# A transformer layer on one core: where the next chunk's residual work stands in the FFN stage

## The reference

```python
x = layernorm(x + attention(x))      # 8 heads of 64, 2 key heads, partial rotary, gated, projected by Wo
h = x @ W1.T + gate * (x @ v.T @ fast_b.T @ u.T)   # W1: ternary weights times a scale, 1024 hidden
r = relu(h)
x = layernorm(x + (r * r) @ W2.T)    # W2: ternary weights times a scale
```

## Time and profile before

| | us |
|---|---|
| median of 3 runs | 1777.85 |
| lowest, highest | 1777.14, 1778.02 |
| the profiled execution | 1775.12 |
| its span in the profile | 1773.3 |
| TensorE busy | 1670.2 (94%) |
| VectorE busy | 1390.5 (78%) |
| GpSimd busy | 989.9 (56%) |
| ScalarE busy | 742.0 (42%) |
| mean granted TensorE clock | 0.972 |

### The profile page before, as it was taken

The page is one execution under the profiler, slowest core; times in us unless marked ns, Lnnn a source line. Parts: engine busy times, 40 slices in busy tenths (PEclk is TensorE's granted clock), DMA queues, the critical chain, the costliest instruction groups (busy, mean ns, idle before and its releaser), DMA issues.

```text
span 1773.3 us, 26408 instructions
## 1 busy us (share of the span) xinstructions
PE 1670.2 (94%) x6902; PEld 817.4 (46%) x6902; DVE 1390.5 (78%) x1692; ACT 742.0 (42%) x1407; POOL 989.9 (56%) x765
## 2 busy tenths in 40 slices
PE   5699999999999999999868999999999999999996
PEld 3444444444444444447744444444444444444585
DVE  6668888888888888757766788888888888885587
ACT  1244444444444444444422444444444444445352
POOL 0546666666666665653334566666666666657342
PEclk8799999999999999999987999999999999999998
DMA  4600101000000000020043010000000000000001
GB/s 163 159 18 23 23 23 24 22 22 22 23 22 22 22 20 19 1 78 24 25 115 84 18 29 23 23 23 22 22 22 23 22 22 22 19 1 1 25 25 48
DMA packets 36916, 59.76 MB, mean 34 GB/s; under 512 B 6624, under 2 KB 17264, under 8 KB 36288
## 3 DMA queue, kind: packets, MB, share of 16 engines
q1 hardware_dynamic: 36800, 58.50, 12.6%
HBM read 20.07 MB, written 4.19 MB: 14 GB/s over the span
## 4 chain that ended last, share of the span: by engine, by line
PE 75%; DVE 10%; issue 8%; ACT 2%; DMA 2%; POOL 1%; SPq 1%; DVEq 0%; ACTq 0%; POOLq 0%
PE ob L578 24%; PE trio L566 16%; PE trio L567 11%; PE sc L533 8%; PE trio L513 6%; PE trio L672 3%; DVE acc L328 2%; PE trio L589 2%; DVE maxp L1059 2%; PE sc L639 2%; ACT probs L824 2%; DMA acc<-in_x 1%; PE ob L687 1%; PE trio L687 1%; PE trio L525 1%
## 5 line engine op out<-in xcount | busy, mean ns | idle before, releaser
L328 POOL TENSOR_TENSOR acc<-acc,probs 128x512 f32<-128x512 f32 x448 | 577.2, 1288 | 435.1 <-DVE acc L328 377.2
L824 ACT ACTIVATE probs<-trio 128x512 f32<-128x512 f32 x1024 | 530.0, 603 | 654.5 <-PE trio L567 556.4
L1059 DVE TENSOR_REDUCE maxp<-sc 128x2 f32<-128x1024 f32 x472 | 575.1, 1218 | 138.6 <-PE sc L535 137.1
L578 PE MATMUL ob<-probs,v_sb 128*64 128x512 f32 x2048 | 495.8, 605 | 0.0
L328 DVE TENSOR_TENSOR acc<-acc,probs 128x512 f32<-128x512 f32 x448 | 429.9, 960 | 81.3 <-ACT probs L824 76.7
L566 PE MATMUL trio<-qa,kab 128*128 128x512 f32 x1024 | 459.8, 449 | 3.6 <-DMA qb<-mrow 3.6
L567 PE MATMUL trio<-qb,kab 128*128 128x512 f32 x1024 | 405.0, 396 | 0.0
L566 PEld LDWEIGHTS trio<-qa,kab 128*128 128x128 f32 x1024 | 192.4, 188 | 322.6 <-issue 210.7
L578 PEld LDWEIGHTS ob<-probs,v_sb 128*64 128x64 f32 x2048 | 123.9, 136 | 241.6 <-issue 178.8
L533 PE MATMUL sc<-kab,qa 64*128 64x512 f32 x512 | 197.1, 460 | 29.1 <-DVE maxp L1198 16.0
L567 PEld LDWEIGHTS trio<-qb,kab 128*128 128x128 f32 x1024 | 194.1, 190 | 23.4
(11 more groups left out here) (122 smaller groups left out, 1420.4 us busy)
## 6 DMA issues: line engine op xcount, KB each, us to landing
qa<-high_sb SPq DMA_DIRECT2D x128, 128.0 KB, 2.3
qb<-low_sb SPq DMA_DIRECT2D x64, 128.0 KB, 2.3
tables_sb<-in_tables SPq DMA_DIRECT2D x34, 128.0 KB, 2.4
xT_sb<-in_xT SPq DMA_DIRECT2D x2, 2048.0 KB, 10.2
acc<-in_x SPq DMA_DIRECT2D x8, 512.0 KB, 4.2
out_y<-acc SPq DMA_DIRECT2D x8, 512.0 KB, 3.1
kab<-acc SPq DMA_DIRECT2D x24, 128.0 KB, 2.4
rot_sb<-raw_sb SPq DMA_DIRECT2D x72, 32.0 KB, 1.8
```

The lines of the kernel that those rows point to most:

```text
L328: ops.tensor_tensor(total, total, part, ALU.add).then_inc(summed, 1)
L578: mm = nc.tensor.matmul(ob[hd * D:(hd + 1) * D, :], v_sb[:, t, kv * D:(kv + 1) * D], probs[:, t % RING, hd * CHUNK:(hd + 1) * CHUNK], star ...
L824: nc.scalar.activation(probs[:, t % RING, hd * CHUNK:(hd + 1) * CHUNK], score_bank(t, hd), ACT.Exp, scale=float(D) ** -0.5).then_inc(probs ...
L1059: nc.vector.tensor_reduce(two_columns(p, j), MAX_PAIRS[j % 2], AX_X, ALU.max).then_inc(maxed, 1)
```

## The change

Three engines get a new order in the FFN stage; no instruction is added or left out. On SyncE the residual load of chunk c + 2 is issued ahead of the wait for chunk c's second norm and of its store. On TensorE the output transposes of chunk c + 1 stand ahead of `ffn_up(c)`. On VectorE `first_norm` is cut in three: the residual adds of chunk c + 1 run right behind `split_x1(c)`, its statistics behind split 5, and only its normalise stays at the end of the iteration.

```diff
--- before.py
+++ after.py
@@ -466,10 +466,10 @@
                 load_residual(1)
                 for c in range(NCH):
                     n = b * NCH + c
+                    if c + 2 < NCH:
+                        load_residual(c + 2)
                     sp.wait_ge(post_done, done(n + 1))
                     sp.dma_start(out_tiles[:, n, :, :], yout).then_inc(y_stored, 16)
-                    if c + 2 < NCH:
-                        load_residual(c + 2)
             sp.wait_ge(y_stored, 16 * (BATCH * NCH + 1))
 
 
@@ -752,9 +752,9 @@
                 x1_transposes(first_n, x1s[0], (first_n + 2) * HC)
                 pe.wait_ge(w_split, done(4 * (b + 1)))
                 for c in range(NCH):
-                    ffn_up(first_n + c)
                     if c + 1 < NCH:
                         output_transposes(first_n + c + 1)
+                    ffn_up(first_n + c)
                     if c + 2 < NCH:
                         if c + 2 == NCH - 1:
                             pe.wait_ge(og_step, done(2 * UNITS * (b + 1)))
@@ -1141,7 +1141,7 @@
                         last.then_inc(signal, 1)
                 return last
 
-            def first_norm(n, c, count):
+            def residual_add(n):
 
                 dve.wait_ge(xres_loaded, 16 * (n + 1))
                 for i in range(TILES):
@@ -1149,8 +1149,13 @@
                         dve.wait_ge(tr_ready, done(2 * n + i // 2 + 1))
                     nc.vector.tensor_tensor(y1[:, i, :], sc[:, 2 + i // 2, (i % 2) * HID:(i % 2 + 1) * HID],
                                             xres[:, i, :], ALU.add).then_inc(res_done, 1)
+
+            def first_stats(n, count):
+
                 dve.wait_ge(res_done, done((n + 1) * TILES))
                 variances(count, y1)
+
+            def first_norm(c, count):
                 normalise(count, y1, x1s[c % 2], x1_done)
 
             def second_sum(n, c, count):
@@ -1217,18 +1222,24 @@
                 for q in range(PARTS):
                     reciprocal(b, NCH - 1, PAIRS - 1, q)
                 count = 2 * NCH * b
-                first_norm(b * NCH, 0, count)
+                residual_add(b * NCH)
+                first_stats(b * NCH, count)
+                first_norm(0, count)
                 for c in range(NCH):
                     n = b * NCH + c
                     split_x1(n)
+                    if c + 1 < NCH:
+                        residual_add(n + 1)
                     if c >= 1:
                         second_sum(n - 1, c - 1, count + 2 * c)
                     for j in range(JT):
                         split_square(n, j)
                         if j == JT // 2 - 1 and c >= 1:
                             second_norm(n - 1, count + 2 * c)
+                        if j == JT - 3 and c + 1 < NCH:
+                            first_stats(n + 1, count + 2 * c + 1)
                     if c + 1 < NCH:
-                        first_norm(n + 1, c + 1, count + 2 * c + 1)
+                        first_norm(c + 1, count + 2 * c + 1)
                 second_sum((b + 1) * NCH - 1, NCH - 1, count + 2 * NCH - 1)
                 second_norm((b + 1) * NCH - 1, count + 2 * NCH - 1)
```

## The result

The changed kernel took 1764.87 us (median of 4 runs, 1764.74 to 1767.65), the kernel before beside it 1777.49 (4 runs, 1777.04 to 1778.02): a ratio of 0.9933, 95% interval 0.9915 to 0.9950. On another chip it was 1766.03 (6 runs) beside 1775.97 (11 runs): 0.9947, 0.9935 to 0.9959. The two differences are 12.6 and 9.9 us. The forecast was 1771.8, a gain of 6.1, with a range from 1766.5; the direction was right, the gain larger than the range allowed.

The account below looks back on a forecast made before the run. TensorE bounds the kernel (75% of the span), waiting for VectorE's normalise in the FFN. Per batch 0.95 - 0.75 + 2.65 + 0.2 = 3.05, two batches 6.1, giving 1771.8 us; 8-in-10 range 1766.5 to 1777.7.

Parts of the forecast that it names:

- Loads ahead of the store: SyncE's queue: residual loads no longer wait behind the store, so VectorE's 2.92 us load wait vanishes.
- c = 0: FFN iteration 0: TensorE's up projection starts with inputs ready; gain 0.95 us per batch, bounds 0.5 and 1.0.
- c = 1: FFN iteration 1: pause before chunk 2 goes, +0.65; relu 4 waits for split 0, costing 1.4; net -0.75 us per batch.
- c = 2: FFN iteration 2, decided by VectorE's sum: 4.64 - 2.25 - 1.85 + 2.1, net gain 2.65 us per batch.
- one add for each square: Rival, chance 0.13: second-sum adds each wait for one square, 3.75 us longer; stall 3.2 in c = 1; 1779.2 us.
- Clock after the pause: TensorE's clock still falls late in the 3.2 us pause before chunk 3: +0.2 us per batch, bounds -0.3 and +1.75.
- the clock holds: Rival, chance 0.18: 3.2 us of pause before chunk 3 leaves the clock up; each batch gains 1.75; 1768.6 us.
- attention is untouched: Attention, outside the changed FFN stage: the change was taken to gain or lose nothing there.
- The base of the sum: Profiled execution 1775.12 us gave 1769.0; the gain was applied to the runs' median 1777.85, 2.73 above, giving 1771.8.

Follow-up runs that it names:

- the late adds without the moved transposes: Changed kernel with residual adds moved behind split 5, just ahead of the statistics, and TensorE's order as before: 1766.10 us, 0.9944 to the kernel before.
- the late second norm: Changed kernel with residual adds behind split 5 and the second norm behind the first, with own buffers: 1760.23 us, 0.9913 to the kernel before.

## Why the prediction was too small

**Loads ahead of the store: right.** VectorE waits for a residual load only in the first chunk of each batch, and alone the step gave 3.0 per batch in c = 2 and the pause of about 0.7 in c = 1.

**c = 0: right.** +0.84 (mean of three profiles before and after) against +0.95; the ends that the prediction itself gives, 804.52 and 803.6, make 0.9.

**c = 1: right, by the wait that was named.** -0.65 against -0.75. Relu 4 waits for split 0. The stall costs 1.34 (28.46 against 27.12 in the kernels without it; 1.03 of it is idle in the row above), forecast 1.4.

**c = 2: right.** +2.80 against +2.65. The adds took 3.02 (1.42 + 1.85 = 3.27 forecast), the second sum started 2.10 later than before, counted from the transposes of the normed chunk (849.48 - 844.75 against 847.69 - 845.06), forecast 2.25; and the first four splits and the norm took 1.29 + 2.13 + 3.35 = 6.77 where 5.8 + 2.62 stood, 1.65 given back, forecast 2.1.

The rival "one add for each square" falls: four adds took 3.02, not 5.2. The Trainium skill, "SBUF — State Buffer", section "Who interferes with whom", has the two block each other for the whole instruction, and the trace agrees when the four adds are taken one by one. Adds and squares in order of their starts:

```profile
850.65 1.04 POOL L983 TENSOR_TENSOR raw_sb<-raw_sb 128x512 f32<-128x512 f32 x1 [16.12 <-ACT raw_sb L865]
850.81 1.17 DVE L1170 TENSOR_TENSOR oge<-oge,probs 128x256 f32<-128x256 f32 x1
851.90 0.41 DVE L1170 TENSOR_TENSOR oge<-oge,probs 128x256 f32<-128x256 f32 x1
852.03 1.18 POOL L983 TENSOR_TENSOR raw_sb<-raw_sb 128x512 f32<-128x512 f32 x1 [0.34 <-ACT raw_sb L865]
852.23 1.26 DVE L1170 TENSOR_TENSOR oge<-oge,probs 128x256 f32<-128x256 f32 x1
853.39 1.33 POOL L983 TENSOR_TENSOR v_sb<-v_sb 128x512 f32<-128x512 f32 x1 [0.18 <-ACT v_sb L865]
853.41 0.41 DVE L1170 TENSOR_TENSOR oge<-oge,probs 128x256 f32<-128x256 f32 x1
```

The first and third add (1.17, 1.26) end 0.3 behind the square under way, the second and fourth take 0.41, as alone, and the squares beside those take 1.18 and 1.33 instead of 1.04. So what the rival had wrong was not the blocking but the count: two adds pass for each square that they wait for, and the next square is held up in turn.

**Clock after the pause: nearly right.** The pause came out as 3.11, forecast 3.2. Tails were 4.28, 2.82, 4.42, 4.42, 5.18 and 4.30 in the six pauses of the three profiles, a mean of 4.24 against 4.21 before; forecast a gain of 0.2. The rival "the clock holds" came true in one pause of six. Stretches of the changed kernel's first profile: the tail of batch 0, then the end of the pause and the tail of batch 1:

```profile
869.59:873.87 4.28, 4.28 (x25) 4.28 (x25) 1.66 (x3) 1.17 (x2) 0.00 (x0) 0.63 0.00 0
1728.00:1731.31 3.31, 0.20 (x2) 0.00 (x1) 3.15 (x11) 0.21 (x1) 0.00 (x0) 1.00 0.00 0
1731.31:1734.13 2.82, 2.82 (x24) 2.82 (x25) 1.38 (x3) 1.08 (x2) 0.00 (x0) 1.00 0.00 0
```

In sum the stage gained 5.9 (two batches), forecast 6.1.

**The step that failed is "attention is untouched".** It put a term at nothing because the order of that work stays; the order stays, its clock does not, and by the means of three profiles that gave 1.9 us in the heads and 3.2 in attention of batch 1, nearly as much as the FFN. The heads: in the kernel before, batch 1, and in the changed one, batch 1, the same matmuls (length, busy, clock third from the end):

```profile
1639.60:1658.75 19.15, 17.80 (x44) 7.53 (x44) 9.41 (x24) 4.67 (x8) 7.38 (x6) 0.91 0.16 55
```

```profile
1635.05:1652.74 17.69, 16.10 (x45) 6.94 (x45) 9.41 (x24) 4.64 (x8) 7.39 (x6) 1.00 0.18 59
```

With the clock down for part of the stretch it is 1.5 longer. Then attention of batch 1: its first 18 us, its start up to the score product (L533) that lies some 668 us before its end, and all of the rest. The kernel before:

```profile
897.66:915.66 18.00, 13.60 (x31) 6.13 (x32) 9.98 (x23) 4.84 (x8) 2.84 (x2) 0.81 0.33 106
...
897.66:966.18 68.52, 47.00 (x162) 25.84 (x163) 40.16 (x52) 15.16 (x27) 27.06 (x21) 0.75 0.49 119
966.18:1634.01 667.83, 663.19 (x2672) 288.77 (x2672) 550.66 (x577) 299.51 (x576) 414.36 (x318) 1.00 0.08 20
```

The changed kernel, third profile:

```profile
897.75:915.75 18.00, 15.68 (x54) 8.47 (x55) 11.37 (x26) 6.04 (x10) 3.25 (x3) 0.91 0.42 126
...
897.75:961.25 63.50, 45.11 (x163) 24.80 (x163) 38.22 (x52) 15.25 (x27) 27.28 (x21) 0.76 0.52 129
961.25:1629.07 667.82, 663.12 (x2673) 288.81 (x2672) 550.64 (x577) 299.50 (x576) 414.40 (x318) 1.00 0.08 20
```

The same 162 or 163 matmuls took 68.52 and 63.50 us, and the 667.8 behind them agree to 0.01. The mean clock of the start is nearly the same, 0.75 and 0.76; by these means it was at 0.50 for some 34 us in the one and 30 in the other. The rest of the difference is which work the low stretches fall on. In the first 18 us, at 0.81, TensorE did 31 matmuls; at 0.91, 54. The other two profiles after, rows of the first and of the second, did 40 at 0.91 and 56 at 1.00:

```profile
894.55:912.55 18.00, 14.10 (x40) 6.88 (x41) 10.86 (x23) 4.84 (x8) 3.77 (x3) 0.91 0.37 116
894.55:961.46 66.91, 46.23 (x162) 24.53 (x163) 40.03 (x51) 15.18 (x27) 27.06 (x21) 0.74 0.49 122
```

```profile
895.36:913.36 18.00, 14.15 (x56) 8.06 (x56) 11.31 (x25) 6.04 (x10) 3.63 (x3) 1.00 0.43 127
895.36:960.27 64.91, 44.67 (x162) 25.07 (x162) 38.01 (x51) 15.48 (x27) 27.51 (x21) 0.79 0.51 126
```

All fourteen profiles of this study fall in line: where TensorE did 28 to 36 matmuls in those 18 us, attention took 735.9 to 737.4 (nine profiles); where it did 40, 734.9 (one); where it did 52 to 56, 731.3 to 734.1 (four). From 5.5 to 13 us after the first L513 the clock was 0.54 to 0.58 in eight of the nine, 0.77 in the ninth and in the one, and 1.00 in the four.

Attention of batch 1 took 735.9 to 736.6 in all seven profiles that keep VectorE's old order (three before, the loads alone, the transposes alone, both, the added memset), and 731.3 to 737.4 in the seven with a new one. Heads of batch 1 were 19.15 or 19.16 in all seven of the first kind, and in two of the seven of the second (the late adds without the moved transposes, and the late second norm); heads of batch 0 took either value in both kinds. So with the old order batch 1 met nearly the same clock in every profile, and with the new one it varies from run to run and is on average better (734.1 against 736.3). What ties the clock of batch 1 to the order in batch 0's FFN is open. It is not the fall in the pause before chunk 3: the late second norm kept 1.00 there and had the long start (attention 736.15), the second changed profile fell (tail 4.42) and had a short one. Nor did the one shift of the code that was tried move it, nor is it the chip: on one and the same chip the old order gave 736.42 and 736.57, the new one 731.32 and 734.12. That a change of order moves the clock elsewhere by up to 5 us is shown by seven profiles against seven; how it does so, and that one could aim for it, is not.

The base of the sum played a part too: the profiled execution before lay 2.73 below the median to which its gain was applied. Against the profiled executions alone the gain was 10.4, against the medians 12.6 and 9.9. For the 2.2 between 10.4 and 12.6 there is no trace: the runs of the kernel before that stand beside it (1777.04 to 1778.02) left none.

## What to carry to other kernels

Try the parts of a change one by one and compare stages, not totals: loads and transposes gave 7.5 us in the FFN and the whole change 5.9, since work put ahead of a ring's consumers (the residual adds) cost 1.34 per batch. Look for what still stands on the line that the pause waits for and that nobody needs: the norm of the chunk before was worth 1.7 in c = 2 of each batch, and behind the shorter pause that it left the clock stayed at 1.00; the early statistics were worth 0.3. Where a kernel's clock falls in short stretches, allow a change anywhere in it some us either way, and read the granted clock in stages that the change does not touch.

## What was not expected of the hardware

- One and the same kernel spread from 1771.27 to 1778.74 us over its runs, some 0.4%.
- The same matmuls at nearly the same mean clock (0.75, 0.76) took 68.5 or 63.5 us.
- A pause of TensorE of 3.11 us was followed by a tail of 2.82 in one case and of 4.28 to 5.18 in five; one of 2.88 by 2.82 in both batches. A pause of only 1.8 us lies ahead of every head, and in 14 of 28 heads, those of 19.15, the clock fell to 0.50 soon behind it.
- The adds beside squares slowed by a factor of 2.1 (1.42 to 3.02), all of it in two of the four (1.17 and 1.26), while the statistics (L1120, L1124 of the changed kernel) stayed at 0.43 there.
